# A quantum-circuit branch beside a feed-forward stage: the circuit's inputs of batches 1 to 7 move from eight TensorE products to chained multiply-reduces on VectorE

## The reference, cut to what matters

```python
def L0(x, vol, w1, b1, w2, b2, pd_w, pd_b, vqc_w, pu_w, pu_b, q_scale, ln_g, ln_b):
    ffn_out = x + gelu(x @ w1 + b1) @ w2 + b2              # 512 -> 2048 -> 512
    p = clip(x @ pd_w + pd_b, -10, 10)                     # 512 -> 4, the circuit's inputs
    q_in = sigmoid(p) * PI
    q_out = vqc(q_in.reshape(-1, 4), vqc_w).reshape(B, T, 4)
    xq = x + (q_out @ pu_w + pu_b) * abs(q_scale)
    out = where(vol > 0.5, xq, ffn_out)                    # per batch
    return layernorm(out) * ln_g + ln_b
```

## Time and profile before

| | |
|---|---|
| median of 3 runs | 2437.83 us (2432.8 to 2438.77) |
| profiled execution | 2438.72 us, span 2436.9 us |
| PE busy | 2378.8 us, 98% of the span |
| DVE busy | 1356.6 us, 56% |
| ACT / POOL busy | 1011.8 us / 1017.2 us, 42% each |
| PE, the group L994 and L995 | 32 instructions each, a matmul of 389 ns |
| DVE, L839 (`hl`) | 256 instructions, 908 ns on average |
| one batch of the first stage | 94.0 us |

### The profile page before, as it was taken

How to read it: one execution, slowest core, us unless ns; L and a number is a source line. 1 busy time by engine, 2 the same in 40 slices (tenths; PEclk the granted TensorE clock), 3 DMA queues, 4 the chain that set the end, 5 groups by cost and what they waited for, 6 DMA issues and landing times. The chain is left out here.

```text
span 2436.9 us, 44424 instructions
## 1 busy us (share of the span) xinstructions
PE 2378.8 (98%) x16068; PEld 1903.5 (78%) x16068; DVE 1356.6 (56%) x2749; ACT 1011.8 (42%) x2057; POOL 1017.2 (42%) x829
## 2 busy tenths in 40 slices
PE   8999999999999899999999999997999999999999
PEld 6788888888887677777777777776888888888887
DVE  7355454454465777776777777778443333333322
ACT  6132232232242766766666676767321211211111
POOL 0042242341334886767676676767022112202200
PEclk9999999999999999999999999998999999999999
DMA  7110110101133455565556566565320110110100
GB/s 227 44 44 18 47 55 18 43 34 43 43 96 113 148 186 183 178 198 152 192 161 197 154 193 191 172 190 178 117 82 1 52 52 0 52 52 0 52 35 18
DMA packets 141841, 244.21 MB, mean 100 GB/s; under 512 B 13756, under 2 KB 28236, under 8 KB 141664
## 3 DMA queue, kind: packets, MB, share of 16 engines
q1 hardware_dynamic: 141664, 241.92, 31.1%
HBM read 216.69 MB, written 25.20 MB: 99 GB/s over the span
## 5 line engine op out<-in xcount | busy, mean ns | idle before, releaser
L1219 POOL TENSOR_TENSOR at_bias<-at_bias,at_mask 128x512 f32<-128x512 f32 x512 | 593.2, 1186 | 261.9 <-DMA at_bias<-in_fside_Bx16xSxS 241.6
L645 ACT ACTIVATE L_hid<-bank,L_b1c 128x512 f32<-128x512 f32 x256 | 176.6, 690 | 964.3 <-PE bank L290 964.3
L837 DVE CAST L_hh<-L_hid 128x512 fp32r<-128x512 f32 x256 | 123.6, 483 | 747.4 <-PE bank L946 713.8
L288 PE MATMUL bank<-xth,L_w1h 128*128 128x512 f32 x1024 | 403.3, 394 | 1.4 <-DVE xtl L730 1.4
L944 PE MATMUL bank<-L_w2h,L_hh 128*128 128x512 f32 x1024 | 401.5, 392 | 0.0
L289 PE MATMUL bank<-xth,L_w1l 128*128 128x512 f32 x1024 | 399.9, 391 | 0.0
L290 PE MATMUL bank<-xtl,L_w1h 128*128 128x512 f32 x1024 | 399.6, 390 | 0.0
L946 PE MATMUL bank<-L_w2l,L_hh 128*128 128x512 f32 x1024 | 399.1, 390 | 0.0
L945 PE MATMUL bank<-L_w2h,L_hl 128*128 128x512 f32 x1024 | 398.9, 390 | 0.0
L1275 ACT ACTIVATE at_bias<-at_bias,cos_sin 128x512 f32<-128x512 f32 x512 | 363.2, 713 | 9.0 <-DVE cos_sin L1411 8.9
L1411 DVE CUSTOM_DVE_ANT_0 at_bias<-bank,at_bias 128x512 f32<-128x512 f32 x512 | 332.6, 684 | 37.1 <-PE bank L1592 25.9
(11 more groups left out here) (205 smaller groups left out, 3238.9 us busy)
## 6 DMA issues: line engine op xcount, KB each, us to landing
at_bias<-in_fside_Bx16xSxS SPq DMA_DIRECT2D x256, 512.0 KB, 3.7
L_ring<-in_L_cond_w SPq DMA_DIRECT2D x32, 256.0 KB, 4.5
L_xres<-in_x SPq DMA_DIRECT2D x8, 1024.0 KB, 5.3
x_scratch<-L_xres SPq DMA_DIRECT2D x8, 1024.0 KB, 4.3
at_xres<-x_scratch SPq DMA_DIRECT2D x8, 1024.0 KB, 7.4
L_xin<-x_scratch SPq DMA_DIRECT2D x8, 1024.0 KB, 5.6
L_xres<-x_scratch SPq DMA_DIRECT2D x8, 1024.0 KB, 5.6
L_xin<-in_x SPq DMA_DIRECT2D x7, 1024.0 KB, 5.3
```

What stands on the lines that cost most here:

```text
L288: nc_mm = pe.matmul(out, ah, bh, start=i == 0, stop=False)
L645: nc.scalar.activation(hid[m % 2][:, :], turn[m % 2][:, :], func, bias=b1c[:, m:m + 1]).then_inc(h_act, 1)
L1219: nc.gpsimd.tensor_tensor(tile, tile, mask[:, m % TT, :], ALU.add).then_inc(masked, 1)
```

## The change

For batches 1 to 7 the inputs of the circuit are computed a batch ahead on DVE, from `xin` (x of the next batch by rows, which is in SBUF for the transposes anyway): for each of 4 row tiles and 4 wires one `tensor_tensor_reduce` multiplies 512 columns of x by one column of `pd_w` and sums them into one element of `angle`. The weights lie in a new tile `pd_across`, [128, 512, 4], all of `pd_w` in every partition, where `w_pass` was; a DMA of SP fills it in the first batch once the second embedding product is done. `pd_across[:, :, w]` reads every fourth word. Each reduce waits for the one before. They stand in m = 8 to 11 (one row tile for each m) of batches 1 to 6, in m = 12 to 15 of batch 0, and in batch 7 there are none. Batch 0's own inputs are computed on PE as before. The products `inputs`, ACT's copy, PE's turn at m = 2 and `circuit_inputs` go from batches 1 to 7. PE's wait for `up_added` moves from the batch's start to m = 9. Two loads of the attention stage wait for `p_out` instead of `ada_mm` and `p_mm`.

```diff
-        pt = at(PT, "pt", [2 * WIRES, S])
+        pt, unused = at(PT, "pt", [2 * WIRES, S]), at(PT, "unused", [P, S])
+        pd_across = at(W_PASS, "pd_across", [P, D, WIRES])
+        pd_in = sem("pd_in")
...
             if l0 and first:
                 setup.load_wada(sp, 1)
+                sp.wait_ge(setup.ada_mm, 2)
+                across_all = t["L0_cond_pd_w"].rearrange("d w -> (d w)").partition_broadcast(P)
+                sp.dma_start(pd_across[:, :, :].rearrange("p d w -> p (d w)"), across_all).then_inc(pd_in, 16)
                 setup.store_rows(sp)
...
-                if l0 and not first:
-                    inputs()
...
+        def next_inputs(b, i):
+
+            if i == 0:
+                wait_apart(dve, passed_dve, (x_in, b * 16), (pd_in, 16))
+            for w in range(WIRES):
+                if i or w:
+                    wait_apart(dve, passed_dve, (dve_chain, link.base + link.n))
+                link.step(nc.vector.tensor_tensor_reduce(unused[:, :], xin[:, i, :], pd_across[:, :, w], 1.0, 0.0, ALU.mult, ALU.add,
+                                                         angle[:, i, w:w + 1]))
+            if i == TT - 1:
+                link.wait()
+                link(nc.vector.tensor_tensor(angle[:, :, :], angle[:, :, :],
+                                             pdb[:, :].unsqueeze(1).to_broadcast([P, TT, WIRES]), ALU.add))
+                nc.vector.tensor_scalar(angle[:, :, :], angle[:, :, :], 10.0, -10.0, ALU.min, ALU.max).then_inc(p_out, 1)
...
                     if l0:
-                        if m == 3:
+                        if m == 3 and first:
                             circuit_inputs(b)
+                        start = 12 if first else 8
+                        if start <= m < start + TT and not last:
+                            next_inputs(b + 1, m - start)
                         if m == 5:
                             circuit_angles(b)
                         if m == 7:
...
-            if m == 2:
-                if not first:
-                    pe.wait_ge(up_added, b * TT)
-                wait_apart(pe, passed_pe, (pt_out, b + 1))
+            if m == 2 and first:
+                pe.wait_ge(pt_out, 1)
...
             if m == 9:
+                if not first:
+                    pe.wait_ge(up_added, b * TT)
                 pe.wait_ge(amp_out, b * 4 + 4)
...
                     pe.wait_ge(xt_lo, b * KT + KT)
-                    if not first:
-                        pe.wait_ge(up_added, b * TT)
-                        inputs()
...
             load_weights(0)
-            sp.wait_ge(s0["ada_mm"], 2)
+            sp.wait_ge(s0["p_out"], B)
             load_weights(1)
-            sp.wait_ge(s0["p_mm"], B)
```

More of the change, by code:

```diff
@@ L825, in body @@
                 if l0:
-                    links = 1 + 2 + 1 + 4 + (0 if first else 4 * TT)
-                    link.at(ahead if first else ahead + 8 + (b - 1) * (8 + 4 * TT))
+                    following = 0 if last else TT * WIRES + 1
+                    links = 1 + (2 if first else 0) + 1 + 4 + (0 if first else 4 * TT) + following
+                    rest = TT * WIRES + 1
+                    link.at(ahead if first else ahead + 8 + rest + (b - 1) * (6 + 4 * TT + rest))
                 else:
@@ L1039, in ffn_stage @@
     if l0:
-        sems.update(row_set=row_set, row_added=row_added, p_mm=p_mm, up_added=up_added, ada_mm=setup.ada_mm)
+        sems.update(row_set=row_set, row_added=row_added, p_out=p_out, up_added=up_added)
     return {"sync": on_sync, "gpsimd": on_gpsimd, "scalar": on_scalar, "vector": on_vector, "tensor": on_tensor, "sems": sems}
```

## The result

The changed kernel takes 2499.01 us at the median of 4 runs (2493.58 to 2500.35), beside 2436.71 us for the kernel before: a ratio of 1.0253, with a 95% interval of 1.0233 to 1.0274. It is **slower by 2.5%**. The forecast was 2482 us in 2434 to 2524. The profiled execution has a span of 2496.6 us, 59.7 more than before. The part of the kernel behind the first stage is the same work in every run here, and in the profiled executions it still takes between 1678.6 us (e9) and 1687.5 us (e10), counted from batch 7's first product of `stack` to the end. One execution of e9, at 2944.45 us with a mean granted clock of 0.751, is left out of its ratio.

What follows compares the result with a forecast made beforehand. PE, busy 98% of the span, bounds the kernel. 5.0 + 6 x (7.3 + 1.8 - 2.25) - 2.25 = +43.9 on 2438.72 gives 2482.6; the median lies 0.9 lower, so 2482 us, range 2434 to 2524.

Steps and rivals of the forecast that it cites:

- PE's gain: Batch start and m = 2: products and small transposes leave PE, 2.25 us in each of seven batches, 15.75 us.
- The place of the loss: m = 11 to 12, b = 1 to 6: L779 queues on DVE behind the reduces and PE waits for it.
- The reduce: Each DVE multiply-reduce: 1.00 us to the end of its read plus 0.10 to the next start, 1.10 apiece.
- POOL's row adds: 365.49 to 371.15 us in b = 3: about 0.95 us more per DVE operation with two SBUF operands.
- The wait: PE at m = 12 waits for L779 from 373.79 to 381.1, a stall of 7.3 us in b = 1 to 6.
- The clock: Behind each PE wait of b = 1 to 6: slower matmuls, 1.8 us charged, taken from the program's start.
- Batch 0: m = 12 to 15: DVE slips 0.5 us three times, PE's transposes wait for xtl, 5.0 us once.
- The sum: Whole kernel: 5.0 + 41.1 - 2.25 = +43.9 us on the profiled 2438.72, so 2482.6; median 2482 us.
- A: Rival on the reduces: the strided operand costs nothing, 0.74 to 0.84 us apiece, 2433 to 2444 us; chance 0.23.
- B: Rival on the reduces: the read is slower still, up to 1.76 us apiece, about 2520 to 2557 us; chance 0.17.
- C: Rival at m = 12: faster, L779 not held and PE's 2.25 us a batch gained, 2424 us; chance 0.11.
- D: Rival: long stall in the first batch or long weight DMA, but the loop even, 2440 to 2450; chance 0.07.

Runs made afterwards that it cites:

- e9: The change with row tiles at m = 8, 9, 12, 13 (batch 0: 12, 12, 13, 14), weights wire by wire, two alternating product buffers: 2431.21 us.
- e10: As e9, but the DMA turning the weights in DRAM is issued as 512 rows of four words: 2420.9 us, ratio 0.9925 to the kernel before.
- e1: The change without its sixteen reduces, so part of the output is not computed: 2422.53 us, ratio 0.9949 to the kernel before.
- e3: The change with circuit_halves moved ahead of the four reduces at m = 11: 2472.54 us, ratio 1.0151 to the kernel before.
- e4: The change with the loop's row tiles at m = 8, 9, 12 and 13 instead of 8 to 11: 2431.41 us, ratio 0.9974.
- e2: The change with reduces reading 512 adjacent weight words instead of every fourth, giving another output: 2451.65 us, ratio 1.0056 to the kernel before.
- e8: The change with 34 extra PE matmuls at m = 12 of batches 1 to 6, before the wait: 2488.45 us, ratio 1.0215.

## Why the prediction was right

- **What bounds the kernel, and PE's gain.** PE at 94.00 of 94.0 us, 2.25 us a batch. e1's batch is 91.64 us, 2.42 less than 94.06, and its time 2422.5, where 15.75 less than the median gives 2421. Right, and 0.17 a batch too small.
- **The place of the loss.** L779 behind the reduces of m = 11, PE's product at m = 12 waiting for it, in b = 1 to 6. Six waits are there, e3 takes away 5.2 us of each by order at m = 11 alone, and e4 all of it by moving half of the reduces. Right.
- **The reduce**, taken as 1.10 us from start to start. It measured 1.07 for the operation and its read, where I took 1.00, and 0.19 to 0.20 idle behind three out of four, where I took 0.10 behind each: 4.8 us for four that follow each other, 1.20 apiece, beside 4.4. This is the term that was too small. The gap had its row, 0.15 before L719, and I should have used it. That the operation came out near 1.00 was luck as far as the row goes: the 1.00 is the mean of L839 alone at 0.69 and L839 beside POOL at 1.66, and has nothing to do with a step, while e2 shows 0.69 for the reduce once the words are adjacent, as the earlier trace rows had it. The Trainium skill, "Vector Engine (DVE) Microarchitecture Reference", section 5.2, gave 1.73 ns a column for one source that hops 4 KiB at every element, an estimated 1.04 us; here, at a step of four words, it is 1.07 with the step and 0.69 without, so the trace agrees. Its slower case, 2.50 (both sources or the output stepping 24 words), did not come up with one source at a step of four words.
- **POOL's row adds.** I took about 0.95 us more for an operation beside them: the two reduces of m = 10 took 1.08 and 0.81 more. Right. The cast of m = 10 I had at 0.91; it took 1.51, 0.6 more than in the sum.
- **The wait**, 7.3 us forecast, is 9.35. In b = 1 the sixteen reduces are 1.7 us longer than in the sum and the cast of m = 10 is 0.6; the other steps differ by 0.2 or less.
- **The clock**, 1.8 us from the program's start, is 2.3 for each wait by the batches' lengths, and e8 gives back 10.6 us for the six. Right in kind and a little small. Batch 0's wait has a cold clock too, 1.7 us, which I had not charged.
- **Batch 0**, 5.0 us forecast, is 6.7. By its own terms the sum should have read 4.3: from cast(15) at 110.3, 1.12 + 4.4 + 0.4 + 0.65 lead to 116.9 for the first xtl, not 117.6. What it missed is the reduces' size: DVE slipped 0.8, 0.9 and 1.2 us in the three m, where I had 0.5 each. The weights' DMA landed 4.7 us after its issue, in time.
- **The sum with the measured terms**: 6.7 + 1.7 + 6 x (9.35 + 2.3 - 2.42) - 2.42 = 61.4, which is what the first stage grew by; it closes because the clock's terms come from the same batches. Against the +43.9 of the sum that is 17.5 more: 12.3 from the six waits, 3 from their clock, 3.4 from batch 0, less 1.2 for PE's larger gain.
- **The rivals.** A (the step costs nothing) is what e2 runs: 2451.65 us, where the forecast said 2444 for it; the wait of 3.0 us was right (3.2), "hardly a cold clock" was not (2.2 us a wait). B needed a slower read than 1.07. C would have needed another place for L779, as e4 has. D's stall is there, 6.7 us in batch 0, but the loop is not even.

## What to carry to other kernels

An engine that is half idle on average can still be the wrong place for new work: lay the added instructions, in their order, against the one instruction in that engine's queue that the bound engine waits for next, and count from the last moment at which the queue was free. Look at the order first: with the same reduces the kernel takes 67.6 us more in one order than in another, and in the better one they cost the batches of the loop nothing (91.64 us with and without them). When an operation walks a tile with a step, lay the tile out so that it doesn't; and when a chain of equal operations waits only because of a scratch output that nobody reads, give it two buffers.

## What the runs showed of the hardware that I had not expected

- A wait of PE of 3.0 us (e2) is already followed by a granted clock of 0.50, and so is one of 4.2 us (e3); one of 1.69 us (e8) is not. Of e8's two waits of 2.01 us one is (0.52) and one is not. e2's batches last 13.3 us beyond 91.64 and their waits, 2.2 a wait, beside 2.3 in the change for waits three times as long. A short wait on PE costs more in clock, share for share, than a long one.
- Under POOL's adds the reduce with a step took 2.15 and 1.88 us in b = 1, 1.08 and 0.81 on top of its 1.07, where the cast and hl beside them took 1.08 and 0.97 more: the two surcharges add up.
- An 8 KB DMA within DRAM held up 1 MB loads issued behind it. Where it was written as four long rows (e9), a load issued 20 us later still took 19.2 us instead of 5; as 512 rows of four words (e10), only the two right behind it were late (15.3 and 15.0 us).
